# The tensor engine reads the expert number of the next tile behind the sixth of twelve matmuls instead of ahead of the tile's first one

## The reference

```
x = layernorm(x + attention(x))          # time mix, k v r projections, a scan over time, output projection
logits = xt @ wg                         # xt: 4096 tokens x 512, wg: 512 x 8
gate, idx = max(softmax(logits)), argmax(logits)
out = gate * (xt @ W[idx] + b[idx])      # W: 8 x 512 x 512
x = layernorm(x + out)
```

## Time and profile before

| | us |
|---|---|
| median of 3 runs | 676.62 |
| the runs | 675.92, 676.62, 677.89 |
| the profiled execution | 679.24 |
| its span, first to last instruction | 677.3 |
| mean granted clock of TensorE, as a share of full speed | 0.938 |
| third stage, end of the last matmul | 663.98 |

### The profile page before, as it was taken

How to read it: one execution, slowest core, us unless ns; L and a number is a source line. 1 busy time by engine, 2 the same in 40 slices (tenths; PEclk the granted TensorE clock), 3 DMA queues, 4 the chain that set the end, 5 groups by cost and what they waited for, 6 DMA issues and landing times. The chain is left out here.

```text
span 677.3 us, 8986 instructions
## 1 busy us (share of the span) xinstructions
PE 591.4 (87%) x2484; PEld 438.7 (65%) x2485; DVE 554.9 (82%) x866; ACT 403.9 (60%) x735; POOL 307.3 (45%) x230
## 2 busy tenths in 40 slices
PE   0576788999999999999999999998665999899992
PEld 0355665676778667668768767855464777676771
DVE  7948899998999999999999899678956566566661
ACT  3346475477567656756757647566331677577773
POOL 4743544443551552463444444248304356465541
PEclk9679899999999999999999999898955899899997
DMA  8030010031022013104104103392204576577650
GB/s 309 3 124 1 0 63 0 2 109 62 16 84 72 32 33 122 31 0 155 31 0 148 41 0 125 137 382 103 59 20 140 147 219 211 184 218 216 213 174 6
DMA packets 36562, 67.60 MB, mean 100 GB/s; under 512 B 8560, under 2 KB 8560, under 8 KB 36532
## 3 DMA queue, kind: packets, MB, share of 16 engines
q1 hardware_dynamic: 30292, 48.29, 21.8%
q0 software_dynamic: 6240, 18.94, 9.0%
HBM read 50.17 MB, written 18.88 MB: 102 GB/s over the span
## 5 line engine op out<-in xcount | busy, mean ns | idle before, releaser
L971 POOL TENSOR_TENSOR mixed<-unsplit,mixed 128x1024 fp32r<-128x1024 f32 x44 | 104.5, 2396 | 133.7 <-ACT mixed L657 133.7
L447 PE MATMUL kb<-mixed,w_kvr 128*128 128x512 f32 x384 | 97.9, 405 | 24.4 <-DVE mixed L1312 16.5
L447 PE MATMUL vb<-mixed,w_kvr 128*128 128x512 f32 x384 | 103.1, 420 | 14.9 <-DVE evn L1150 8.6
L629 PE MATMUL y_ps<-w_e_hi,xgT 128*128 x312 | 110.1, 415 | 3.2 <-issue 1.7
L447 PE MATMUL rb<-mixed,w_kvr 128*128 128x512 f32 x384 | 101.8, 415 | 5.5 <-DVE ee L1164 3.6
L447 PEld LDWEIGHTS kb<-mixed,w_kvr 128*128 128x128 f32 x384 | 73.7, 195 | 43.1 <-issue 16.2
L465 PE MATMUL y_ps<-w_o,rw 128*128 128x512 f32 x224 | 100.7, 592 | 0.0
L447 PEld LDWEIGHTS vb<-mixed,w_kvr 128*128 128x128 f32 x384 | 74.5, 198 | 36.8 <-DVE evn L1150 11.8
L447 PEld LDWEIGHTS rb<-mixed,w_kvr 128*128 128x128 f32 x384 | 73.3, 193 | 27.2 <-issue 6.2
L1101 DVE SCALAR_TENSOR_TENSOR unsplit<-diff,vec,xb 128x512 f32<-128x512 f32 x96 | 74.2, 834 | 7.9 <-PE kb L447 6.0
L981 POOL TENSOR_TENSOR ee<-ee,state 128x512 f32<-128x512 f32 x32 | 35.0, 1093 | 95.6 <-DVE state L1134 94.9
(11 more groups left out here) (198 smaller groups left out, 1052.4 us busy)
## 6 DMA issues: line engine op xcount, KB each, us to landing
bias<-b_experts SPq DMA_DIRECT2D x39, 256.0 KB, 3.6
w_e_raw<-w_experts SPq DMA_DIRECT2D x8, 1024.0 KB, 11.9
rows<-x SPq DMA_DIRECT2D x28, 256.0 KB, 2.6
x_rows<-rows SPq DMA_DIRECT2D x28, 256.0 KB, 2.1
xb<-xT SPq DMA_DIRECT2D x4, 1026.0 KB, 5.3
xb<-xT SPq DMA_DIRECT2D x3, 1024.0 KB, 5.3
w_raw<-w_square SPq DMA_DIRECT2D x2, 1024.0 KB, 10.1
xb<-xT SPq DMA_DIRECT2D x2, 512.0 KB, 5.0
```

The source lines that it names most:

```text
L447: mm = pe.matmul(bank, w_kvr[m][:, a, h, o:o + P], mixed[m][:, bb, h, :], start=(k == 0), stop=(k == 3 * CH - 1))
L629: mm = pe.matmul(y_ps[:, parity, :], xgT[:, third, a, c, :], w[:, bass.ds(e, 1), c, :].rearrange("p u o -> p (u o)"), start=(c == 0 and (a ...
L971: pool.tensor_tensor(mixed[m][:, LO, 2 * hp:2 * hp + 2, :], unsplit[m][:, LO, 2 * hp:2 * hp + 2, :], mixed[m][:, HI, 2 * hp:2 * hp + 2, :] ...
```

## The change

The function `expert_of(k)` holds the read. `expert(k, n, e, ahead)` takes the expert number as an argument and, where `ahead` is set, calls `expert_of(k + 1)` behind the third matmul of the second piece (c == 1), the sixth of twelve, and returns it for the next tile. The first tile's read stands behind the first two `turn` calls; in the loop, each round reads the number of its first tile at its head, in front of that tile's `turn`, and so does the last part. All other instructions, waits and their order stay.

```diff
-            def expert(k, n):
+            def expert_of(k):
+                return pe.value_load(tile_ei[0:1, bass.ds(k, 1)], min_val=0, max_val=EXPERTS - 1)
+
+            def expert(k, n, e, ahead=False):
+
                 parity, third = n % 2, n % 3
-
-                e = pe.value_load(tile_ei[0:1, bass.ds(k, 1)], min_val=0, max_val=EXPERTS - 1)
+                following = None
                 pe.wait_ge(turned_lo, k + 1)
                 pe.wait_ge(y_taken, k + (TILES + 1))
                 for c in range(CH):
@@
                                        start=(c == 0 and (a, w) == (HI, w_e_hi)), stop=(c == CH - 1 and a == LO))
+                    if c == 1 and ahead:
+                        following = expert_of(k + 1)
                 mm.then_inc(expert_filled, 1)
+                return following
 
             pe.wait_ge(tiles_ready, 1)
             turn(0, 0, 0)
             turn(1, 0, 1)
+            e = expert_of(0)
             for k in range(2 * RING):
                 turn(k + 2, (k + 2) // RING, (k + 2) % RING)
                 if k < EXPERTS:
                     expert_ready(pe, k)
-                expert(k, k % RING)
+                e = expert(k, k % RING, e, ahead=k + 1 < 2 * RING)
             with pe.Fori(2, SORTED // RING) as r:
+                e = expert_of(r * RING)
                 for n in range(RING):
                     turn(r * RING + (n + 2), r + (n + 2) // RING, (n + 2) % RING)
-                    expert(r * RING + n, n)
+                    e = expert(r * RING + n, n, e, ahead=n + 1 < RING)
+            e = expert_of(SORTED // RING * RING)
             for k in range(SORTED // RING * RING, SORTED):
                 if k + 2 < SORTED:
                     turn(k + 2, (k + 2) // RING, (k + 2) % RING)
-                expert(k, k % RING)
+                e = expert(k, k % RING, e, ahead=k + 1 < SORTED)
```

## The result

Twenty runs of each kernel: 672.8 us median (669.19 to 676.09) behind the change, 677.02 (673.91 to 682.99) before it. The ratio is 0.9932, its 95% interval 0.9911 to 0.9953, so the change takes away 3.2 to 6.0 us. The profiled execution's span is 671.9 us, 5.4 less than before.

What follows compares the result with a forecast made beforehand. TensorE bounds the routed stage (119.7 of 126 us busy), the gather loop nearly level at 3.27 against 3.22 us a tile. Gain 4.6 less 0.3 is 4.3; 676.62 - 4.3 = 672.3 us, range 669.6 to 675.2.

Steps and rivals of the forecast that it cites:

- The read costs only behind a late gather: Expert-number read on TensorE's sequencer: costs nothing when the gather is early, up to 0.6 us when it lands late.
- the argument from tile 7 alone: Tile 7's read starts 0.2 us behind the late gather's landing, so the sequencer is held; 0.48 us lost there.
- 7.1 us of idle time go: Weight loads before expert matmuls: issue idle time of 7.1 us in 16 places falls to under 1.5.
- Part of it comes back as waits for gathers: Routed stage: the gather loop limits the gain to between 3.1 and 7.1 us.
- the 3.1 I had as the lower bound: Gain if gathers bound all the time: 0.5 us in each of 5.5 rounds, plus 0.4 at the first tile.
- One sign of the prediction: Transposes' waits for gathers in the profile after: stay near 5 us or grow by up to 3.
- Another: Gather landing times in the profile after: a median over 4.4 us would show the prediction wrong.
- The price of a longer loop of gathers: Rival that gathers take the gain back: each 0.1 us more landing time costs 0.55 us; 675.1, chance 0.11.
- The cover in the middle: Read behind the sixth matmul: just hidden, a 567 ns read sticks out by up to 0.25 us; 0.3 taken off.
- the 0.6 us for issuing six matmuls: Late tile with an empty queue: sixth matmul issued at 0.6 us at the latest, counted from the first.
- Tile 0: First tile's read: the next transposes hide some 0.6 us of its delay, so about 0.4 us stays to be won.
- The 4.6 us: Gain chosen for the routed stage between 3.1 and 7.1 us, before 0.3 off for reads that stick out.

Runs made afterwards that it cites:

- the run with memsets: Changed kernel with two GpSimd memsets, each waited for, in front of every gather into a used slot: 682.59 us, ratio 1.0101.
- AHEAD 6: AHEAD 6 instead of 5, so gathers are issued one tile earlier: changed kernel 663.58 us, kernel before 665.32 us.
- the kernel with AHEAD 6 and memsets: Changed kernel with AHEAD 6 plus two GpSimd memsets in front of each gather into a used slot: 665.91 us, repeated 665.9.

## Why the prediction held, and which of its steps didn't

- **The read costs only behind a late gather.** Held, and shown from both sides: with early gathers both kernels have the same stage to 0.01 us, and with the read doubled in front the idle time before expert matmuls doubles, from 7.1 to 15.4 us. The prediction set the Trainium skill (Perfetto Trace Analysis, section Sequencer Loop) against this: an engine instruction is pushed into a queue and waits there for its semaphore. The trace disagrees where that rule applies, in the tiles that are written out. At tile 9 of the kernel before, the weight load that waits for the gather and the read behind it start together, at 556.05:

```profile
556.05 0.31 PEld L618 LDWEIGHTS kb<-ident,xg 128*128 128x128 f32 x3 [0.46 <-DMA xg<-x_rows,ids]
...
L624 PEldq TENSOR_LOAD <-tile_ei x1: 301/301/301, 556.1 to 556.1; - x1
```

But 11 of the 16 places lie in the loop, and there the rule doesn't bear on it. The wait for the gather is carried by a register operation of the sequencer itself (L78, as its operands in the trace say), so the sequencer has to stand. At tile 24:

```profile
L78 PEldq FUSED_REGOPS  x1: 42/42/42, 612.3 to 612.3; - x1
...
L624 PEldq TENSOR_LOAD <-tile_ei x1: 312/312/312, 612.5 to 612.5; - x1
```

So the argument from tile 7 alone was narrower than the prediction took it: for most late tiles the two agree.
- **7.1 us of idle time go.** Held: none is left in front of expert matmuls.
- **Part of it comes back as waits for gathers.** Held in kind. With 121.6 us as the stage without any wait (measured, not only worked out now), the kernel before lost 134.8 - 121.6 = 13.2 us: 6.7 to the read (7.1 less tile 0's 0.4), 1.4 to the lower clock at tile 16, 5.1 to gathers. The changed kernel lost 131.1 - 121.6 = 9.5, all to gathers. So in this pair of executions 4.4 of 6.7 us came back as waits for gathers, and 2.3 stayed won, with tile 0 2.7. That is less than the 3.1 I had as the lower bound; the medians say 4.2, with an interval from 3.2 to 6.0. One execution of each can't tell a gather's luck from the change, and I leave the term at that: between the two bounds by the medians, below them by the pair of profiles. One sign of the prediction missed: the waits of transposes were to grow by at most 3 us, and on the weight-load row they went from 5.7 to 13.9, on the matmul row from 3.0 to 6.4. Another can't be read: the profile of the changed kernel gives no landing times. In the kernel with two reads in the middle their median is 4.0 us, as before.
- **The price of a longer loop of gathers.** I put each us of landing time at 5.5 us. In the run with memsets a gather came some 1.4 us later in all, which makes 7.7 us; the stage of its profile grew by 8.0. By the medians it was 10 to 11 us, or 7 to 8 us for each us, so the price may be too low by up to half. What I left out I can only argue: on ACT the norm of tile k stands behind the copy of the transposed tile k + 3, so a late gather also holds back the next gather of a tile before it. No run takes this apart.
- **The cover in the middle was mis-sized, to the good side.** I had the sequencer ready for the seventh matmul 1.4 us behind the first, just in time, and took 0.3 us off for long reads. In tile 14 above the first matmul starts at 572.77 and the bound test of the read ends at 573.73, 0.96 behind; the seventh is due at 1.48 (574.01 + 0.24). The step that failed is the 0.6 us for issuing six matmuls: the read begins at 573.1, only 0.3 behind the first matmul. The sequencer was early because it doesn't start with the first matmul: its first address operation of the tile (L632) stands at 572.5, when the transposes have just begun. So the 0.3 us shouldn't have been taken off: no expert matmul of the changed kernel waits for its weights, although its longest read takes 571 ns.
- **Tile 0.** From the transposes of tile 2 to the first expert matmul it was 523.64 - 522.55 = 1.09 us; in the changed kernel they start at 521.08 and 521.81, 0.73 apart. So 0.36 us, where I had about 0.4. Held.

The forecast of 672.3 met 672.8. The mechanism is shown, but that the number is so near is in part luck. The 4.6 us were a choice between 3.1 and 7.1, the 0.3 taken off were wrong, and the median before moved by 0.4 us from three runs to twenty. The measured gain is itself known only from 3.2 to 6.0 us.

## What to carry to other kernels

In this kernel a sequencer instruction behind the wait for a transfer stood on the path from the landing to the first matmul (0.83 us at tile 7); in front of the wait it ran beside matmuls that were already issued (0.40 us at tile 14). So look at what the trace shows between the releasing wait and the first instruction of the engine, and move reads of registers ahead of the wait, not merely "earlier". And before moving them ask why the wait is late: here one number that issues the gathers a tile earlier brought, alone, about two and a half times the change (1.7 to 1.9% against 0.7%), and left some 0.4 us at tile 0 as all that the place of the read is worth.

## What the runs showed of the hardware

- TensorE's clock rises at different points of tile 0. In the profile of the changed kernel all twelve matmuls ran 0.43 us apart (521.81 to 526.65); in that of the same kernel with AHEAD 6 the pace turned to some 0.24 from 523.70 on. From the first transposes of tile 0 to those ahead of tile 1 the two took 8.6 and 7.1 us, and two executions of the kernel before with AHEAD 6 took 8.6 and 8.2. So tile 0, whose code is the same in all of them but for the read, takes up to 1.5 us more or less from one execution to the next.
- 14 matmuls of 5.2 us in all raised the granted clock from 0.50 to 1.00. In the 3.4 us without a matmul behind them it fell back, and the transposes that followed ran at 0.50.
- A weight load that waited for a gather held back the sequencer's next instruction: at tile 9 both start at 556.05.
- In the kernel with AHEAD 6 and memsets, at 231 GB/s instead of 207, the gathers landed later: 4.9 us median, up to 5.7, against 4.0 in the earlier trace rows. In that execution no transposes waited for them behind tile 0.
